# Two attention layers on one core: on-chip norms, split transfers and a new order of the engines' queues

## The reference

```python
# layer 1, cut
q, k_t, v_t = heads(x @ W_q), heads(text @ W_k), heads(text @ W_v)
probs_t = softmax(q k_t * scale)
text_out = probs_t v_t
attn_scores = q k_ip * scale                    # 4 image tokens
qsem = _l2norm(einsum('bhst,bte->bhse', probs_t, text))
sem = einsum('bhse,bne->bhsn', qsem, _l2norm(ip))
probs_ip = softmax(attn_scores + 0.5 * sem) * spatial_mask
x = (text_out + probs_ip v_ip) @ W_out + b_out + x
```

## Time and profile before

| what | value |
|---|---|
| median of 3 runs | 2473.29 us (2472.25 to 2475.6) |
| profiled execution | 2473.34 us, span 2471.8 us |
| PE busy | 2273.8 us, 92% of the span |
| DVE, ACT, POOL busy | 1699.8, 1726.8, 1593.7 us |
| share of the 16 DMA engines, hardware queue | 44.0% |
| granted TensorE clock, mean | 0.98 |

### The profile page before, as it was taken

The page is one execution under the profiler, slowest core; times in us unless marked ns, Lnnn a source line. Parts: engine busy times, 40 slices in busy tenths (PEclk is TensorE's granted clock), DMA queues, the critical chain, the costliest instruction groups (busy, mean ns, idle before and its releaser), DMA issues.

```text
span 2471.8 us, 90321 instructions
## 1 busy us (share of the span) xinstructions
PE 2273.8 (92%) x35896; PEld 1458.5 (59%) x35896; DVE 1699.8 (69%) x2860; ACT 1726.8 (70%) x2602; POOL 1593.7 (64%) x1056
## 2 busy tenths in 40 slices
PE   7899967999999999999999999999999999999984
PEld 5677744555555555556555555655556555556552
DVE  5534333777777777777777777777777777777763
ACT  3323325877777777778777778877787787787862
POOL 3212124777777777777777777777777777777762
PEclk9999978999999999999999999999999999999997
DMA  9677642444434444444444444444444444444431
GB/s 289 197 225 229 198 115 64 112 114 115 111 109 117 115 114 117 115 118 116 112 117 116 114 115 119 117 111 116 114 118 116 113 118 118 115 118 117 112 90 56
DMA packets 337787, 310.89 MB, mean 126 GB/s; under 512 B 180208, under 2 KB 280816, under 8 KB 337392
## 3 DMA queue, kind: packets, MB, share of 16 engines
q1 hardware_dynamic: 337392, 305.36, 44.0%
HBM read 164.66 MB, written 105.98 MB: 109 GB/s over the span
## 4 chain that ended last, share of the span: by engine, by line
PE 34%; DVE 18%; DMA 12%; ACT 8%; issue 6%; SPq 6%; POOL 1%; ACTq 0%; DVEq 0%; POOLq 0%
PE psum L933 8%; PE psum L1032 8%; DMA den<-ust 8%; PE psum L1016 6%; PE psum L995 5%; ACT ef L1121 5%; DVE mneg L1180 3%; DVE e L1202 2%; PE psum L936 2%; DVE sq L1221 2%; DVE ust L1269 2%; DVE outt L1280 2%; DMA pt<-p_dram 2%; PE psum L999 1%; PE psum L958 1%
## 5 line engine op out<-in xcount | busy, mean ns | idle before, releaser
L1348 POOL TENSOR_TENSOR e<-ef,eh 73x1024 f32<-73x1024 f32 x320 | 681.4, 2130 | 298.9 <-ACT eh L1136 261.9
L1121 ACT ACTIVATE ef<-psum 73x1024 f32<-73x1024 f32 (+1 forms) x640 | 628.5, 1012 | 104.8 <-PE psum L999 100.9
L1202 DVE TENSOR_TENSOR e<-psum,e 73x1024 f32<-73x1024 f32 x320 | 386.6, 1208 | 158.5 <-PE psum L1032 158.2
L1180 DVE TENSOR_REDUCE mneg<-psum 128x8 f16<-128x616 f32 (+3 forms) x512 | 448.2, 930 | 31.0 <-PE psum L958 30.2
L1032 PE MATMUL psum<-eh,gram 128*73 128x512 f16 x1280 | 337.6, 387 | 36.6 <-ACT ef L1121 12.7
L1016 PE MATMUL psum<-ef,values 128*32 128x256 f32 x5120 | 363.5, 389 | 8.0 <-DVE pip L1262 5.9
L995 PE MATMUL psum<-q_high,keys 32*73 32x256 f16 (+2 forms) x6144 | 325.5, 259 | 33.9 <-DVE mneg L1180 25.4
L1136 ACT ACTIVATE eh<-ef 73x1024 f16<-73x1024 f32 x320 | 337.0, 1053 | 16.4 <-ACT ef L1121 0.8
L995 PEld LDWEIGHTS psum<-q_high,keys 32*73 32x73 f16 (+1 forms) x6144 | 187.7, 111 | 143.6 <-issue 68.1
L1129 ACT ACTIVATE ust<-psum 128x512 f32<-128x512 f32 x384 | 228.2, 594 | 63.2 <-PE psum L1016 59.2
L1315 POOL TENSOR_TENSOR al<-ust,ah 128x768 f16<-128x768 f32 x128 | 210.7, 1646 | 86.6 <-ACT ah L1159 86.5
(11 more groups left out here) (180 smaller groups left out, 4659.7 us busy)
## 6 DMA issues: line engine op xcount, KB each, us to landing
rb<-r_dram SPq DMA_DIRECT2D x128, 384.0 KB, 3.8
keys<-k_dram SPq DMA_DIRECT2D x128, 231.0 KB, 3.7
values<-v_dram SPq DMA_DIRECT2D x128, 192.5 KB
ust<-ust SPq DMA_DIRECT2D x512, 48.0 KB, 2.1
v_dram<-vst SPq DMA_DIRECT2D x64, 320.0 KB
out<-outt SPq DMA_DIRECT2D x64, 320.0 KB, 2.3
k_dram<-kst SPq DMA_DIRECT2D x32, 616.0 KB, 3.9
x<-in_x SPq DMA_DIRECT2D x32, 384.0 KB, 3.7
```

What stands on the lines that cost most here:

```text
L1121: act.activation(ef[l][0:m, unit_heads(n), :].rearrange("t h s -> t (h s)"), src, ACT.Exp, scale=SM).then_inc(s_exp[l], 1)
L1180: dve.tensor_reduce(dst, o, AX_X, ALU.max, negate=True).then_inc(s_max[l], 1)
L1202: dve.tensor_tensor(rest, banks(l, f"u{k}", 2)[0:m, :, :], rest, ALU.mult).then_inc(s_wr, 1)
L1348: pool.tensor_tensor(e2[0:m, k, :, :], ef[1][0:m, unit_heads(k), :], eh[0:m, unit_heads(k), :], ALU.subtract).then_inc(s_e2, 1)
```

## The change

There are three parts. First, the norms: `ns` is now `move_norms`, four transfers from SBUF to SBUF (6 partitions of `nst` to 24 of `n2` each), and `nl` and `n_dram` are gone. Second, image scores and probabilities: each of the two transfers with three chunks is now three transfers of 32 partitions, and the waits count 16 for each. Third, `ORDER` and `USES` are new: all five queues are in another order, with the five `n` steps of PE in one run, and the banks are given out anew.

```diff
 ORDER = {
     "pe": """
-        1u2/3 1a1/3 0t1/1 1q/2 0t2/1 0a0/1 1s0/2 0a1/1 1s1/2 0a2/1 1i/2 1a2/3 1u3/3 1m/2 1u4/3 1t0/2 0q/0
-        1n0/3 1p/4 1n1/3 1n2/3 0s0/0 1n3/3 1n4/3 0s1/0 1t1/2 1a0/2 1u0/2 1t2/2 1u1/2 1o/4 0m/0 0o/1 0t0/0""",
+        1s1/2 1a1/3 1a2/3 1i/2 1u3/3 1m/2 1u4/3 1t0/2 1n0/3 1n1/3 1n2/3 1n3/3 1n4/3 1p/4 0q/0 1t1/2 1u0/2
+        0s0/0 1t2/2 1u1/2 0s1/0 1o/4 0m/0 0o/1 0t0/0 1u2/2 1a0/2 0t1/0 1q/1 0t2/0 0a0/0 1s0/1 0a1/0 0a2/0""",
     "act": """
-        1a1/3 1f/4 0t2/1 0t3/1 1q/2 0t4/1 1h4/3 0a0/1 0a1/1 0a2/1 1i/2 1a2/3 1m/2 0r/0 1t0/2 1h0/2 0q/0
-        1t1/2 1h1/2 1n/3 1g/4 1t2/2 1t3/2 1a0/2 0g/1 1t4/2 1h2/2 0m/0 1r/2 1h3/2 0t0/0 0t1/0""",
+        0a1/1 0a2/1 1a1/3 1i/2 1a2/3 1m/2 1t0/2 1h0/2 1n/3 1t1/2 1h1/2 1g/4 0q/0 1t2/2 1t3/2 1h2/2 1t4/2
+        0g/1 0r/1 1h3/2 0m/0 1r/2 0t0/0 0t1/0 1a0/2 0t2/0 0t3/0 1f/3 1q/1 0t4/0 0a0/0 1h4/2""",
     "dve": """
-        1y11/4 0o/2 1y12/4 1y13/4 1y14/4 1w2/3 1y15/4 1y16/4 1y17/4 1y18/4 1y19/4 1ql/2 1s0/2 1s1/2 1s2/2
-        1s3/2 1w3/3 0d/1 1w4/3 1d/3 0ql/0 1p/4 0s0/0 0s1/0 0s2/0 0s3/0 1w0/2 1w1/2 1y0/3 1y1/3 1y2/3 1y3/3
-        1o/4 1y4/3 1y5/3 1y6/3 1y7/3 1y8/3 1y9/3 1y10/3""",
+        1ql/2 1s0/2 1s1/2 1s2/2 1s3/2 1w3/3 0d/1 1w4/3 1d/3 1p/4 0ql/0 1w0/2 0s0/0 1y0/3 0s1/0 0s2/0 0s3/0
+        1y1/3 1o/4 1w1/2 1y2/3 1y3/3 1y4/3 0o/1 1y5/3 1y6/3 1y7/3 1y8/3 1y9/3 1y10/3 1w2/2 1y11/3 1y12/3
+        1y13/3 1y14/3 1y15/3 1y16/3 1y17/3 1y18/3 1y19/3""",
     "pool": """
-        1xh/2 1xl/2 1b3/3 1b4/3 0xh/0 0xl/0 1vb/4 1kb/1 1at/4 1c/2 1b0/2 1b1/2 1al/4 0at/1 0al/1 1b2/2""",
+        0xh/0 0xl/0 1b0/2 1b1/2 1al/4 0at/1 0al/1 1b2/2 1c/2 1xh/1 1xl/1 1b3/2 1at/3 1kb/1 1vb/3 1b4/2""",
     "sp": """
-        1ss/3 1sl/3 1rl/4 1sh/4 0x/0 1vi/4 1ps/4 0ds/1 1v/2 1pl/4 1ds/3 0k/0 1g/2 0rw/1 0sh/1 0rl/1 1c/1
-        1ns/3 1rw/3 1nl/3 1k/1 1d/3 1st/4 0v/0""",
+        0x/0 0ds/1 1v/2 1pl/4 0k/0 1ds/3 1g/2 0rw/1 0sh/1 0rl/1 1ns/3 1ss/2 1rw/3 0v/0 1d/3 1st/4 1sh/3
+        1rl/3 1k/1 1c/1 1vi/2 1ps/3 1sl/2""",
 }
 
 USES = [
-    "0t3/1 0a0/1 0a2/1 1u3/3 0q/0 0s0/0 0s2/0 1u1/2 0t1/0",
-    "0t3/1 0t4/1 1s1/2 1u3/3 0q/0 0s0/0 0s2/0 1a0/2 1u1/2 0m/0 0t1/0",
-    "1a1/3 0t4/1 1s1/2 1i/2 1u4/3 1n/3 1t2/2 1u0/2 1o/4",
-    "0t2/1 0t4/1 1s0/2 1s3/2 1u4/3 1p/4 1t2/2 1u0/2 1o/4 0t0/0",
-    "0t2/1 0t4/1 1s0/2 1s3/2 1t0/2 1p/4 0s3/0 1t4/2 0t0/0",
-    "1u2/3 1q/2 1s2/2 1t0/2 1p/4 0s3/0 1t4/2 0o/1",
-    "1u2/3 1q/2 1s2/2 1t1/2 0s1/0 1t3/2 1t4/2 0o/1",
-    "0a1/1 1a2/3 1m/2 1t1/2 0s1/0 1t3/2 1t4/2 1y/3",
+    "1a1/3 1m/2 1t0/2 0q/0 0s1/0 0s3/0 1y/3 0a1/0",
+    "1a2/3 1t0/2 0q/0 0s1/0 0s3/0 0m/0 0t0/0 0t2/0 0a0/0 0a2/0",
+    "1i/2 1u4/3 1p/4 1t2/2 0s0/0 1u1/2 0t0/0 0t2/0 0t4/0 1s1/1",
+    "1u4/3 1p/4 1t2/2 0s0/0 1u1/2 1a0/2 0t4/0 1s1/1",
+    "1s2/2 1u3/3 1p/4 1t3/2 1t4/2 1o/4 0t1/0 0t3/0 0t4/0 1s0/1",
+    "1s2/2 1u3/3 1n/3 1t3/2 1t4/2 1o/4 0t1/0 0t3/0 0t4/0 1s0/1",
+    "1s3/2 1t1/2 1u0/2 1t4/2 0s2/0 0o/1 1u2/2 1q/1",
+    "1s3/2 1t1/2 1u0/2 1t4/2 0s2/0 0o/1 1u2/2 1q/1",
 ]
...
-            def store_norms(l, b, n):
+            def move_norms(l, b, n):
                 b.reached(sp, s_n, 1, 1)
-                sp.dma_start(n_dram, nst[:]).then_inc(s_ns, 16)
-
-            def load_norms(l, b, n):
-                b.reached(sp, s_ns, 16, 16)
-                rows = n_dram.rearrange("(j k) n -> j (k n)", j=NJ)[:, 0:2 * CW * S]
-                sp.dma_start(n2[:], rows.rearrange("j (x i) -> j x i", i=QS)).then_inc(s_nl, 16)
+                for j in range(NJ):
+                    rows = nst[j * SLOT:j * SLOT + 2 * CW, :].rearrange("k (q i) -> k q i", i=QS)
+                    sp.dma_start(n2[j * HD:(j + 1) * HD, :], rows).then_inc(s_nl, 16)
 
             def store_ip_scores(l, b, n):
                 b.reached(sp, s_sip, 1, 1)
-                dst = s_dram[b.parity()].rearrange("m (c s) -> c m s", c=CW)
-                sp.dma_start(dst, sipst[:, b.parity(), :]).then_inc(s_ss, 16)
+                for c in range(CW):
+                    sp.dma_start(s_dram[b.parity()][:, c * S:(c + 1) * S], sipst[c * SLOT:(c + 1) * SLOT, b.parity(), :])\
+                      .then_inc(s_ss, 16)
...
             def load_ip_probabilities(l, b, n):
                 b.reached(sp, s_ps, 16, 16)
-                src = p_dram.rearrange("m (c s) -> c m s", c=CW)
-                sp.dma_start(pt[:], src).then_inc(s_pt, 16)
+                for c in range(CW):
+                    sp.dma_start(pt[c * SLOT:(c + 1) * SLOT, :], p_dram[:, c * S:(c + 1) * S]).then_inc(s_pt, 16)
```

More of the change, by code:

```diff
@@ L670, in _, with attention @@
             pool.tensor_tensor(early.xl[:], early.xin[:], early.xh[:], ALU.subtract).then_inc(early.s_xl, 1)
-def attention(nc, psum, early, x, k_dram, v_dram, g_dram, c_dram, kip_dram, vip_dram, r_dram, n_dram, s_dram, p_dram,
+def attention(nc, psum, early, x, k_dram, v_dram, g_dram, c_dram, kip_dram, vip_dram, r_dram, s_dram, p_dram,
               wqs, wos, wqt, wot, rnorm, out):
@@ L734, in attention @@
         s_rw, s_rb = pair("inverses_stored"), pair("inverses_spread")
-        s_ns, s_nl = sem("norms_stored"), sem("norms_loaded")
+        s_nl = sem("norms_moved")
         s_ss, s_sl = sem("ip_scores_stored"), sem("ip_scores_loaded")
@@ L875, in spread_inverses @@
                 sp.dma_start(rb[l][:].rearrange("p c s -> p (c s)"), src).then_inc(s_rb[l], 16)
-            def store_norms(l, b, n):
+            def move_norms(l, b, n):
                 b.reached(sp, s_n, 1, 1)
-                sp.dma_start(n_dram, nst[:]).then_inc(s_ns, 16)
-            def load_norms(l, b, n):
-                b.reached(sp, s_ns, 16, 16)
-                rows = n_dram.rearrange("(j k) n -> j (k n)", j=NJ)[:, 0:2 * CW * S]
-                sp.dma_start(n2[:], rows.rearrange("j (x i) -> j x i", i=QS)).then_inc(s_nl, 16)
+                for j in range(NJ):
+                    rows = nst[j * SLOT:j * SLOT + 2 * CW, :].rearrange("k (q i) -> k q i", i=QS)
+                    sp.dma_start(n2[j * HD:(j + 1) * HD, :], rows).then_inc(s_nl, 16)
             def store_ip_scores(l, b, n):
                 b.reached(sp, s_sip, 1, 1)
-                dst = s_dram[b.parity()].rearrange("m (c s) -> c m s", c=CW)
-                sp.dma_start(dst, sipst[:, b.parity(), :]).then_inc(s_ss, 16)
+                for c in range(CW):
+                    sp.dma_start(s_dram[b.parity()][:, c * S:(c + 1) * S], sipst[c * SLOT:(c + 1) * SLOT, b.parity(), :])\
+                      .then_inc(s_ss, 16)
             def load_ip_scores(l, b, n):
                 b.reached(sp, s_y, STEPS, SIP_READ - STEPS)
-                b.reached(sp, s_ss, 16, 16)
+                b.reached(sp, s_ss, 16 * CW, 16 * CW)
                 src = s_dram[b.parity()].rearrange("(n h) (q i) -> (h q) n i", n=IP, i=QS)
@@ L913, in _ @@
                                "vi": load_vip, "ds": move_denominators, "d": move_semantics, "sh": move_numerators,
-                               "rw": store_inverses, "rl": spread_inverses, "ns": store_norms, "nl": load_norms,
+                               "rw": store_inverses, "rl": spread_inverses, "ns": move_norms,
                                "ss": store_ip_scores, "sl": load_ip_scores, "ps": store_ip_probabilities,
@@ L1066, in attend_ip @@
                 b.reached(pe, s_vb, 1, 1)
-                b.reached(pe, s_pt, 16, 16)
+                b.reached(pe, s_pt, 16 * CW, 16 * CW)
                 for c in range(CW):
@@ L1219, in ip_softmax @@
                 if k == 0:
-                    b.reached(dve, s_nl, 16, 16)
+                    b.reached(dve, s_nl, 16 * NJ, 16 * NJ)
                     ins = dve.tensor_scalar(sq[:], n2[:], 4.0 / GS, 1e-37, ALU.mult, ALU.max)
@@ L1389, in attention_stack_kernel @@
     r_dram = [[dram(f"r_dram{l}_{n}", (HC, 2, CW * S)) for n in (0, 1)] for l in both]
-    n_dram = dram("n_dram", (P, S))
     s_dram = [dram(f"s_dram{n}", (IP * HC, CW * S)) for n in (0, 1)]
@@ L1414, in attention_stack_kernel @@
                         g_dram, c_dram, kip_dram, vip_dram, wqs, wos, wqt, wot, rnorm)
-        attention(nc, psum, early, x, k_dram, v_dram, g_dram, c_dram, kip_dram, vip_dram, r_dram, n_dram, s_dram, p_dram,
+        attention(nc, psum, early, x, k_dram, v_dram, g_dram, c_dram, kip_dram, vip_dram, r_dram, s_dram, p_dram,
                   wqs, wos, wqt, wot, rnorm, out)
```

## The result

The changed kernel takes 2586.8 us (median of 6 runs, 2576.3 to 2597.1) against 2472.0 us before (2467.5 to 2475.6). The ratio is 1.0463, 95% interval 1.0441 to 1.0486: 4.6% slower. The forecast was slower too, but by 70 us, and the time lies above its range of 2443 to 2565 us.

A forecast was written before the change was run, and what follows sets the result against it. PE was taken as the bound, its work a floor. Per iteration 31.84 + 0.25 (bank waits) + 0.92 (lock) = 33.01 us; over 62 iterations +73, less 3 in the drain, from 2473.3 to 2543 us; range 2443 to 2565.

The forecast's parts named there:

- the sign: Whole kernel: slower, given a chance of 0.65, against 0.25 for faster and 0.10 for the same.
- the four banks: PE steps newly tied by the bank list: waits of 2.08 us against 1.83 now, +0.25 us per iteration.
- the lock: y0 on DVE, ahead of 0s1's maximum, waits for POOL's running 0at: 0.92 us per iteration, chance 0.45.
- the bank tie: 1t2's third-chunk step on PE waits for weighting 1w0 until X+3.44: 0.91 us.
- the step on the transfers: SP queue: more issues for norms, scores and probabilities offset by 3.2 us of waiting that goes; balance taken as 0.
- both ends of SP's balance: SP's time per iteration after the new transfers: from -3 to +4 us, said to lie in SP's slack.
- at nothing: Cost of the norms' four on-chip transfers before y0, wanted some 5 us after the norm copy's turn on SP.
- the path by which a late SP entry reaches 0at: Behind a late SP entry are queued denominators, then inverses and their spreading, then POOL's 0at; no cost was added.
- X+3.43: Laid-out start of POOL's 0at, 3.43 us after X, the start of PE's 1t1; it runs to X+5.24.
- delays only the softmax, with 5 us to spare: Kernel before: y0's waiting for POOL was said to hold up the softmax alone, with 5 us to spare.
- the transfers had set the pace: Rival: SP's waiting costs 0.5 us per iteration now, so the change is faster, 2455 us; chance 0.24.
- Late denominators: Rival: 0ds lands late, PE waits 0.5 us at 1n4; 2517 us, with the lock 2574; chance 0.07 including other new waits.

The follow-up runs named there:

- The reduce: Changed kernel with POOL's 1vb moved behind 1c and y0 done by tensor_reduce (factor in the norm copy, floor left out): 2496.6 us, ratio 1.0112.
- half of w0: Changed kernel with 1vb moved behind 1c and y0 as a tensor_reduce, plus weighting w0 doing only one of its two halves: 2487.9 us, ratio 1.0064.
- The reduce in the kernel before: Kernel before with only y0 made a tensor_reduce (factor in the norm copy, floor left out): 2450.9 us, ratio 0.9919.
- 1vb early: Changed kernel with POOL's 1vb moved from behind 1at and 1kb to behind 1c; alone, with y0 still tensor_scalar: 2526.5 us, ratio 1.0227.
- the transfers alone: Kernel before, its order and banks kept, with only the new transfers of norms, scores and probabilities: 2472.4 us, ratio 1.0015.
- both moves: Changed kernel with y0 behind layer 0's maxima and 1vb behind 1c: 2500.0 us, ratio 1.0117; with the old transfers 2508.8 us, ratio 1.0153.
- the order alone: Kernel before with the new ORDER and USES but the old transfers, norms load behind the scores' store on SP: 2597.6 us, ratio 1.051.

## Why the prediction was right and wrong

*Right:* the sign, and the mechanism at the four banks and at y0. The step of the short turned scores waits 0.94 us for 1w0 (0.91 laid out), and y0 ends with POOL's 0at. The reduce shows the lock, half of w0 shows the bank tie.

*Wrong:* the step on the transfers, which took both ends of SP's balance to "lie in SP's slack, since its last entries wait for the end of the softmax anyway". SP's last entries are 1vi, 1ps and 1sl, and this holds only from 1ps on. 1vi stands in front of it and waits for 1vb, the last but one on POOL; in the trace 1vb ends 0.3 to 2.4 us after the softmax (0.5 in the median), and from there SP issues with hardly a wait until the norms. So there was no slack to lie in: the six more issues took SP from 20.5 to 24.6 us of issuing per iteration, and what it brought late held up PE. The same step put the norms "at nothing" with some 5 us of cover; y0 waited for them in 45 of 50 iterations, 0.9 us per iteration, because SP reached them late and because four issues took 3.20 us instead of 2.48. The forecast named the path by which a late SP entry reaches 0at, over the inverses, but laid 0at out from POOL's and ACT's work alone: 0at came at X+4.06 in the median, not at X+3.43.

Wrong as well: that y0 now "delays only the softmax, with 5 us to spare". The reduce in the kernel before gave 17 to 20 us, so y0 reached PE before the change too.

*Its size*, in kernels that differ by one step each:

| kernel | us | step |
|---|---|---|
| before, new transfers, reduce | 2455.5 | |
| new order, y0 behind the maxima, 1vb early, reduce | 2478.6 | +23, the order and its banks |
| y0 in its new place, 1vb early, reduce | 2496.6 | +18, the late norms ahead of a maximum |
| the same with tensor_scalar | 2526.5 | +30, the lock |
| the changed kernel, 1vb behind 1at | 2586.8 | +60, the loops over 1vb |

The forecast had 16 us for the banks (0.25 x 62), 57 for the lock (0.92 x 62), and nothing for the other two. So the term missing is the largest, and the lock was put nearly twice too high. That the sum of the first three steps comes near the forecast's 73 is in part luck: the late norms make up for the lock. The steps also depend on what is left: y0's move is worth 26.5 us with tensor_scalar and 18 with the reduce.

*The rivals:* that the transfers had set the pace is refuted by the transfers alone (1.0015). The lock was met, in 48 of 50 iterations, and not missed through a later 0at, as the rival had it: 0at came later than X+4.0 in 26 of 50, but y0 came later too. Late denominators were not seen as a large PE wait: PE's wait at the `n` steps (L1042) is 5.2 us in all.

Open: why the period after varies from 32.4 to 36.1 us from one iteration to the next. Some issues take long: those of x and x0b 0.40 to 2.12 us, with a median of 0.43. Why they do, and whether this is all of it, is not shown. Open too: which waits make up the 23 us of the order itself, and whether longer y0s are all of the 9 us that the old transfers cost once both moves are made.

## What to carry to other kernels

Lay out a new order not only around the busiest engine: follow the transfer queue once around, and look at its every wait, also the one in front of a transfer of 6 KB. Compare the layout with all iterations of the trace, and not with one that fits. When no engine is full and each one waits, look for a loop through all of them in the chain, and for the one wait whose buffer could be read earlier. An instruction that the profile shows with a widely varying length and a constant least one is waiting for something: ask what ends with it.

## What the runs showed that was not expected

- Four on-chip transfers of 6 KB took 3.20 us to issue (1204.12 in SP's timeline, 0.72 to 0.85 each), longer than the four of 48 KB with 2.48 us, which took the same 2.48 in the changed kernel.
- A DVE instruction of 0.2 us cost this kernel 17 to 20 us as a whole, before the change as well, by the form it was written in: 2468.2 to 2450.9 us. The faster form leaves out the floor of 1e-37, so it computes the same only where no squared norm is that small.
- An order that is as slow as the changed kernel can show y0 at 0.19 us: in the order alone the late norms took the place of the lock.
